# Row maxima turned by one matmul and placed by a transfer, loads as stages of the written schedule, a Newton root with a step less

## The reference, cut to what matters

```
x += tanh(g_xattn[0]) * matmul(fake_quant(layernorm(x)), fake_quant(ctx))
x += tanh(g_ffn[0])   * (h @ W_base.T + b + low-rank adapters through an inverse transform),  h = layernorm(x)
x += tanh(g_xattn[1]) * attention(layernorm(x), ctx)     # 32 query heads of 16, 8 key/value groups, masked softmax over 512 keys
x += tanh(g_ffn[1])   * bitlinear feed-forward(layernorm(x))   # int8-like activations, ternary weights, 512 -> 1376 -> 512
```

## Time and profile before

| | us |
|---|---|
| median of 3 runs | 267.83 (267.61 to 267.91) |
| the profiled execution, its own time | 267.79 |
| its span, first to last instruction | 266.0 |
| PE busy | 246.4 |
| DVE, ACT, POOL busy | 215.1, 185.3, 116.6 |

### The profile page before, as it was taken

One profiled execution on the slowest core, in us unless ns is written; L12 is line 12 of the kernel. 1 busy time (PEld: TensorE's weight loads), 2 busy tenths in 40 slices (PEclk: granted clock), 3 DMA queues, 4 the chain that ended last, 5 costly groups with the idle time before them and its releaser, 6 DMA issues.

```text
span 266.0 us, 4711 instructions
## 1 busy us (share of the span) xinstructions
PE 246.4 (93%) x1482; PEld 120.8 (45%) x1482; DVE 215.1 (81%) x613; ACT 185.3 (70%) x311; POOL 116.6 (44%) x172
## 2 busy tenths in 40 slices
PE   8957697979999999999999999999999999996994
PEld 8622275834733334275334266424334244443442
DVE  2976974779898589796999976899788995889995
ACT  3710549969498998487687767998878988543541
POOL 7003312562233022464888754447989668100000
PEclk9999799999999999999999999999999999999899
DMA  6999985152855800000900380630000000000004
GB/s 174 390 369 415 383 365 124 25 122 27 302 186 132 156 10 0 4 0 26 155 0 0 92 346 2 131 48 0 4 2 0 2 0 1 2 0 0 0 2 158
DMA packets 8146, 27.63 MB, mean 104 GB/s; under 512 B 1402, under 2 KB 4010, under 8 KB 6490
## 3 DMA queue, kind: packets, MB, share of 16 engines
q1 hardware_dynamic: 7690, 21.63, 27.8%
q0 software_dynamic: 288, 5.70, 5.6%
q10 hardware_dynamic: 144, 0.00, 0.0%
HBM read 23.87 MB, written 3.41 MB: 103 GB/s over the span
## 4 chain that ended last, share of the span: by engine, by line
PE 60%; DVE 8%; ACT 4%; issue 3%; DVEq 0%; ACTq 0%
PE bank L776 11%; PE bank L803 10%; PE bank L754 10%; PE bank L779 6%; PE bank L826 5%; PE bank L696 4%; PE bank L844 4%; PE bank L762 3%; PE bank L686 2%; PE bank L811 1%; DVE fs L1280 1%; ACT ternary L955 1%; PE bank L863 1%; ACT big L985 1%; PE bank L677 1%
## 5 line engine op out<-in xcount | busy, mean ns | idle before, releaser
L1215 DVE CUSTOM_DVE_ANT_0 junk<-bank,maskb 128x512 bf16<-128x512 f32 x128 | 83.8, 686 | 13.2 <-PE bank L754 12.8
L985 ACT ACTIVATE big<-bank 128x512 f32<-128x512 f32 x128 | 74.6, 597 | 20.4 <-PE bank L776 14.5
L562 POOL TENSOR_TENSOR big<-big,product 128x512 int32<-128x512 int32 x48 | 61.1, 1274 | 37.4 <-ACT big L985 36.9
L776 PE MATMUL bank<-qst,kst 99*128 99x512 bf16 x128 | 48.9, 383 | 0.2
L754 PE MATMUL bank<-kst,qst 96*128 96x512 bf16 x128 | 48.0, 381 | 0.2 <-DVE mx L1215 0.2
L803 PE MATMUL bank<-big,vp 128*32 128x512 f32 x256 | 30.6, 598 | 0.0
L779 PE MATMUL bank<-ident_b,maskb 128*128 128x512 bf16 x80 | 30.4, 380 | 0.0
L572 POOL TENSOR_TENSOR mx<-mx 128x4 f32<-128x4 f32 x64 | 14.1, 220 | 20.8 <-DVE mx L1215 18.6
L754 PEld LDWEIGHTS bank<-kst,qst 96*128 96x128 bf16 x128 | 12.7, 99 | 22.4 <-issue 12.8
L776 PEld LDWEIGHTS bank<-qst,kst 99*128 99x128 bf16 x128 | 12.4, 97 | 20.7 <-ACT big L985 7.9
L606 POOL TENSOR_SCALAR stage_w<-stage_w,wscale 128x1376 f32<-128x1376 f32 (+1 forms) x12 | 17.7, 1476 | 7.5 <-DVE wscale L1337 7.5
(11 more groups left out here) (183 smaller groups left out, 411.3 us busy)
## 6 DMA issues: line engine op xcount, KB each, us to landing
stage_w<-in_w_down POOLq DMA_DIRECT2D x1, 2816.0 KB, 9.9
stage_w<-in_w_gate SPq DMA_DIRECT2D x1, 2752.0 KB, 21.7
stage_w<-in_w_up POOLq DMA_DIRECT2D x1, 2752.0 KB, 10.3
qst<-q_parts SPq DMA_DIRECT2D x18, 128.0 KB, 4.8
q_parts<-parts SPq DMA_DIRECT2D x12, 128.0 KB
x<-in_x SPq DMA_DIRECT2D x4, 256.0 KB, 12.3
big<-in_ctx SPq DMA_DIRECT2D x4, 256.0 KB, 5.1
big<-in_ctxT SPq DMA_DIRECT2D x4, 256.0 KB, 7.2
```

What stands on the lines that cost most here:

```text
L562: nc.gpsimd.tensor_tensor(p, p, keep[:, nt, KEEP_ST.index(i):KEEP_ST.index(i) + 1, :].broadcast_to([P, HG, P]), ALU.mult).then_inc(kept, 1)
L776: i = mm(o[:, :], kst[0:KM, b, g, s * P:(s + 1) * P], qst[0:KM, tile % 2, g * HG:(g + 1) * HG, :], start=True, stop=by_keep(c, s))
L985: fn(pt[:, c % 4, s, :], o[:, :], ACT.Exp).then_inc(drain(stage), 1)
L1215: v.tensor_tensor_reduce(junk[:, j % 2, :], o[:, :], maskb[:, tb(c // NG)[1], :], 1.0, HIDE, ALU.add, ALU.max, mx[:, c % 3, 0, hh:hh + 1]) ...
```

## The change

Stage `m` becomes one matmul with 12 columns of weights (3 parts x 4 heads) into partitions 0 to 11 of a bank, 128 wide. ACT copies these 12x128 values into a new small tile `mrow` (three slots), and SP issues a transfer of 3 KB from there to rows `KS:KM` of `qst`; the first `t` of the chunk waits for that transfer (`max_placed`) and no longer for the copy. `m` moves to `j = 4c + 8` (`LAG_M = 8`) and `t` to a lag of 12. The identity is held once and read four times over by a broadcast.

The loads become stages of the list, each at a place of its own, some of them cut in pieces (`dft` in 2, `wT` in 4, batch 1's transposed context in 4). The stages that read the split queries and keys back are apart from their stores (`kstack`, `qstack`). The root takes two steps in place of three, the first of them of higher order: for one column 5 instructions and not 6, for three columns 7 and not 9. `oT` on DVE waits for the one before it. All stages are ordered anew.

```diff
-RSQRT_SEED = 519526879.0
+RSQRT_SEED = 520464379.0
+ROOT_G = -0.5 / (2.0 / 3.0) ** 0.4
...
-LAG_T = 11
+LAG_M = 8
+LAG_T = 12
 LAG_PV = 25
...
 PREPARATION = [
...
+    ("load_ctx", 2), ("load_x", 0), ("load_ctx", 0), ("warm", 0, 4, 10), ("load_ctx", 3), ("load_x", 3),
+    ("load_ctx", 1), ("load_x", 1), ("scalars",), ("load_enc",), ("warm", 0, 0, 42), ("load_ctxT", 0), ("products",),
+    ("xstats", 0), ("load_x", 2), ("ln0", 0, 1), ("ln0", 0, 2), ("ln0", 0, 3), ("ln0", 0, 4), ("load_dft", 1),
+    ("ln0", 0, 5), ("load_wkv",), ("load_dft", 0), ("xstats", 1), ("load_ctxT", 1), ("load_adapters",),
+    ("warm", 0, 1, 60), ("load_gate",), ("load_ctxT", 2), ("load_mask",), ("load_bias",), ("load_wT", 0),
+    ("cquant", 0), ("load_wT", 1), ("xstats", 2), ("xstats", 3), ("ln0q", 0), ("ln0", 1, 1), ("load_wT", 2),
+    ("load_wT", 3), ("load_ctxT", 5), ("ln0", 1, 2), ("ln0", 1, 3), ("k", 0, 0), ("load_ones",), ("csum", 0),
+    ("q1T", 0), ("k", 0, 1), ("ln0", 1, 4), ("vones",), ("adapters",), ("load_ctxT", 6), ("ln0", 1, 5), ("ln0q", 1),
+    ("r", 0), ("ln0r", 1), ("p", 0), ("vt",), ("ln1", 0, 0), ("ln0", 2, 5), ("load_ctxT", 4), ("ln1", 0, 1),
+    ("ln1", 0, 2), ("ln0q", 2), ("ln1", 0, 3), ("pick",), ("ln1", 0, 4), ("ln1", 0, 5), ("fabs", 0, 0), ("bias", 0),
+    ("fabs", 0, 1), ("we",), ("hT", 0, 1), ("mask",), ("fabs", 0, 2), ("fabs", 0, 3), ("fsum", 0), ("q1T", 1),
+    ("load_ctxT", 3), ("load_ctxT", 7), ("k", 0, 2), ("y0", 0, 0), ("y0", 0, 1), ("ln0r", 2), ("load_ctx", 4),
+    ("y0", 0, 2), ("y0", 0, 3), ("v", 0, 0), ("y0up", 0), ("fscale", 0), ("ln2", 0, 0), ("ln2", 0, 1), ("ln2", 0, 2),
+    ("r", 1), ("ln2", 0, 3), ("ln2", 0, 4), ("fround", 0, 0), ("load_wq",), ("v", 1, 0), ("ln2", 0, 5), ("k", 0, 3),
+    ("ksplit", 0), ("v", 1, 1), ("kstack", 0), ("k", 1, 0), ("p", 1), ("v", 1, 2), ("hT", 0, 2), ("ln1", 1, 0),
...
 FILL = {
...
+    12: [("bias", 2)], 14: [("qsplit", 1)], 15: [("hT", 2, 1)], 16: [("keepT",)], 17: [("y0", 2, 0)],
+    19: [("y0", 2, 1)], 21: [("y0", 2, 2)], 22: [("qstack", 1)], 24: [("y0", 2, 3), ("fabs", 1, 0)],
...
+    32: [("fround", 1, 0)], 33: [("fclamp", 1, 0), ("hT", 2, 2)], 35: [("load_wo",), ("oT", 0)],
...
+    56: [("fternary", 1, 1), ("y1", 0, 3), ("y1up", 0), ("hT", 3, 1)],
+    57: [("ln3", 0, 0), ("ln3", 0, 1), ("fternary", 1, 2)], 58: [("fternary", 1, 3)], 59: [("qstack", 2)],
+    61: [("fload", 2), ("ln3", 0, 2), ("y0", 3, 0)], 63: [("y0", 3, 1)], 64: [("ln3", 0, 3)], 65: [("y0", 3, 2)],
...
+    84: [("q", 3, 2), ("q", 3, 3), ("qsplit", 3), ("y1", 1, 0), ("y1", 1, 1)], 85: [("qstack", 3)],
...
+    179: [("hidden", 1, 2)], 217: [("oT", 7)], 224: [("y1", 3, 0)], 227: [("aT", 3, 1)], 277: [("fq", 0, 2)],
+    281: [("fq", 0, 3)], 288: [("y1", 3, 1)], 294: [("y1", 3, 2)], 296: [("y1", 3, 3)], 325: [("fq", 1, 0)],
+    334: [("f2T", 0, 0)], 341: [("y1up", 3)], 349: [("gu", 2, 0, 0)], 353: [("gu", 2, 0, 1)], 358: [("fq", 1, 1)],
...
+MROWS = 3
...
-        if (j - LAG_T + 1) % 4 == 0 and 0 <= (j - LAG_T + 1) // 4 < NCHUNK:
-            s.append(("m", (j - LAG_T + 1) // 4))
+        if (j - LAG_M) % 4 == 0 and 0 <= (j - LAG_M) // 4 < NCHUNK:
+            s.append(("m", (j - LAG_M) // 4))
...
+        mrow = sb("mrow", [3 * HG, MROWS, P], BF16)
...
+                elif kind == "m":
+                    c = stage[1]
+                    wait_drained(sp, stage)
+                    sp.dma_start(qst[KS:KM, c // NG % 2, c % NG * HG:(c % NG + 1) * HG, :],
+                                 mrow[:, c % MROWS, :]).then_inc(max_placed[c % MROWS], 16)
...
-                    for hh in range(HG):
-                        i = mm(o[KS:KM, hh * P:(hh + 1) * P], mx_top[:, c % 3, :, hh], ident_b[:, 0, :], start=True, stop=True)
-                    i.then_inc(fill(stage), 1)
+                    mm(o[0:3 * HG, 0:P], mx_top[:, c % 3, :, :].rearrange("p k h -> p (k h)"), ident_b[:, 0, :], start=True,
+                       stop=True).then_inc(fill(stage), 1)
...
-                        wait_drained(pe, ("m", c))
+                        pe.wait_ge(max_placed[c % MROWS], 16 * (c // MROWS + 1))
...
-                    fn(qst[KS:KM, c // NG % 2, c % NG * HG:(c % NG + 1) * HG, :],
-                       o[KS:KM, :].rearrange("p (h n) -> p h n", h=HG), ACT.Copy).then_inc(drain(stage), 1)
+                    if c >= MROWS:
+                        act.wait_ge(max_placed[c % MROWS], 16 * (c // MROWS))
+                    fn(mrow[:, c % MROWS, :], o[0:3 * HG, 0:P], ACT.Copy).then_inc(drain(stage), 1)
...
+                    if k == 3:
+                        link(which, v.scalar_tensor_tensor(out=y, in0=w, scalar=5.0 * ROOT_G ** 2, in1=y, op0=ALU.add, op1=ALU.mult))
+                        after(which)
+                    if k == 4:
+                        link(which, v.scalar_tensor_tensor(out=y, in0=u, scalar=1.5, in1=y, op0=ALU.add, op1=ALU.mult))
...
-                    after(which)
-                    link(which, v.scalar_tensor_tensor(out=y, in0=u, scalar=1.5, in1=y, op0=ALU.add, op1=ALU.mult))
+                    if k == 2:
+                        after(which)
+                        link(which, v.scalar_tensor_tensor(out=w, in0=u, scalar=-10.0 / 3.0 * ROOT_G, in1=u, op0=ALU.add, op1=ALU.mult))
...
```

More of the change, by code:

```diff
@@ L342, in gated_blocks_kernel @@
         ld_x = [sem(f"x_loaded{t}") for t in range(NT)]
-        ld_scal, ld_dft, ld_coef, ld_wT, ld_wq, ld_wkv, ld_wo, ld_mask, ld_bias = (
-            sem(n + "_loaded") for n in ("scalars", "dft", "coefs", "wT", "wq", "wkv", "wo", "mask", "bias"))
+        ld_scal, ld_coef, ld_wq, ld_wkv, ld_wo, ld_mask, ld_bias = (
+            sem(n + "_loaded") for n in ("scalars", "coefs", "wq", "wkv", "wo", "mask", "bias"))
         ld_enc = sem("enc_loaded")
+        ld_dft = [sem(f"dft_loaded{i}") for i in range(KT // 2)]
+        ld_wT = [sem(f"wT_loaded{k}") for k in range(KT)]
         enc_cleared = sem("enc_cleared")
@@ L348, in gated_blocks_kernel @@
         ld_ctx1 = sem("ctx1_loaded")
-        ld_ctxT0 = [sem(f"ctxT0_loaded{k}") for k in range(KT)]
-        ld_ctxT1 = sem("ctxT1_loaded")
+        ld_ctxT = [sem(f"ctxT_loaded{i}") for i in range(B * KT)]
         ld_ffn = [sem(f"ffn_loaded{w}") for w in range(3)]
@@ L388, in gated_blocks_kernel @@
         max_split = sem("max_split")
+        max_placed = [sem(f"max_placed{i}") for i in range(MROWS)]
         pv_done = sem("pv_done")
@@ L457, in _ @@
-            sp.dma_start(dft, dft_in).then_inc(ld_dft, 16)
-            sp.wait_ge(enc_cleared, 1)
-            for half in range(2):
-                sp.dma_start(enc[64 * half:64 * half + RR, :], enc_in).then_inc(ld_enc, 16)
-            sp.dma_start(wT[:, :, :], wT_in).then_inc(ld_wT, 16)
-            sp.dma_start(bias[:, :], bias_in.partition_broadcast(P)).then_inc(ld_bias, 16)
-            for t in range(1, NT):
-                sp.dma_start(x[:, t, :], x_in[:, t, :]).then_inc(ld_x[t], 16)
@@ L465, in _ @@
-            sp.dma_start(wqT[:, :, :], wqT_in).then_inc(ld_wq, 16)
-            sp.dma_start(mask_u8, mask_in).then_inc(ld_mask, 16)
-            sp.dma_start(ctx_T[:, 1], ctxT_in[1]).then_inc(ld_ctxT1, 16)
-            sp.dma_start(ctx_n[:, 1], ctx_in[1]).then_inc(ld_ctx1, 16)
-            sp.wait_ge(minus_ready, 1)
-            for b in range(B):
-                sp.dma_start(kst[KS:KM, b, :, :], minus.broadcast_to([KM - KS, NG, SK])).then_inc(kones_ready, 16)
-            sp.dma_start(stage_w[:, 0:WFF[0][1]], WFF[0][0]).then_inc(ld_ffn[0], 16)
@@ L473, in _ @@
-            sp.dma_start(woT[:, :, :], woT_in).then_inc(ld_wo, 16)
-            for stage in SCHEDULE:
-                kind = stage[0]
-                if kind in ("ksplit", "qsplit"):
+            for stage in SCHEDULE:
+                kind, i = stage[0], (stage[1] if len(stage) > 1 else 0)
+                if kind == "load_x":
+                    sp.dma_start(x[:, i, :], x_in[:, i, :]).then_inc(ld_x[i], 16)
+                elif kind == "load_ctx":
+                    if i < KT:
+                        sp.dma_start(ctx_n[:, 0, i], ctx_in[0, :, i]).then_inc(ld_ctx0[i], 16)
+                    else:
+                        sp.dma_start(ctx_n[:, 1], ctx_in[1]).then_inc(ld_ctx1, 16)
+                elif kind == "load_ctxT":
+                    sp.dma_start(ctx_T[:, i // KT, i % KT], ctxT_in[i // KT, :, i % KT]).then_inc(ld_ctxT[i], 16)
+                elif kind == "load_wkv":
+                    sp.dma_start(wkvT, wkvT_in).then_inc(ld_wkv, 16)
+                elif kind == "load_adapters":
+                    sp.dma_start(coef, coef_in).then_inc(ld_coef, 16)
+                    sp.dma_start(cmask, cmask_in).then_inc(ld_coef, 16)
+                elif kind == "load_dft":
+                    sp.dma_start(dft[:, 2 * i:2 * i + 2], dft_in[:, 2 * i:2 * i + 2]).then_inc(ld_dft[i], 16)
+                elif kind == "load_enc":
+                    sp.wait_ge(enc_cleared, 1)
+                    for half in range(2):
```

(20 more changed lines are left out.)

78 lines of the change are left out of this document (33 added, 45 removed), and 86 rows, old and new, of tables (FILL, PREPARATION).

## The result

The changed kernel takes 271.14 us (median of 4, 270.22 to 271.79), the kernel before 267.72 (median of 4, 267.43 to 267.91): a ratio of 1.0113, 95% interval 1.0079 to 1.0146. Foretold were 261.7 us, range 255.0 to 268.5.

The account below looks back on a forecast made before the run. Bounds taken: loads and long chains up to the first score, PE in the loop, a DVE chain at the end. From 267.79 us: -5.5 + 1.5 + 3.0 + 0.5 - 4.6 - 1.0 = -6.1, so 261.7 us, range 255 to 268.5.

Parts of the forecast that it names:

- the one on SP's queue: Loop: the maxima's transfer stands behind whatever SP issues or waits for; 3.0 us lost, bounds 0 and 6.
- The four matmuls: Stage `m` in the loop: three matmuls fewer in each of 32 chunks, 5.5 us saved, bounds 5.5 and 11.3.
- The new wait in twelve short windows: Loop: `t` waits for copy and transfer where four steps are as short as that path; 1.5 us lost, bounds 0 and 10.
- The reads behind the stores: Loop, after `qstack` 1, 2, 3: transfers behind six query reads land late; 0.2 + 1.5 + 1.9 us, within the 3.0 taken.
- One step less for `keep`: Loop: `t` is a step later and `pv` is not, leaving `keep` less room; 0.5 us lost, bounds 0 and 2.
- The preparation: Up to the first score matmul: reordered loads bring it to 57.5 us; 4.6 us saved in all, bounds -8 and +1.
- The root and the end: Last norm and tail: shorter root 0.2 us, `gu 2` fills PE's wait; 1.0 us saved in all, bounds -3 and +2.
- The slower one: Rival, loop: small transfer takes 3.9 us, each of 12 short windows loses 1.5; 274.7 us, chance 0.14.
- The rival in which the loop gives all back: Rival: loop waits reach 9 or 10 us, or the first score stays at 62.5; 266.2 or 266.3 us, chance 0.15.

Follow-up runs that it names:

- the run with the old lag: Changed kernel with maxima placed by four matmuls and a copy, and LAG_M, LAG_T = 10, 11 as before the change: 276.03 us, ratio 1.0294 to the kernel before.
- the kernel with 72 columns: Changed kernel with the one matmul of the maxima widened from 12 to 72 columns of weights, 60 of them zeros: 268.10 us, ratio 0.9997 to the kernel before.

## Why the prediction was wrong

**The step that failed is the one on SP's queue, in this sentence:** "The 2.75 MB of `fload` come on another queue and share the engines." It was priced at nothing, as if a share of the engines were all that a small transfer needs. The transfer landed 6.54 and 5.64 us after issue, about when the load was in, and not the 2.1 of the sum: 3.20 and 2.71 us of waits at the two places, and 4.8 us of low clock behind them, by loads that are not in SP's queue. With the loads cut to 128 columns the kernel takes 262.1 us. So 9.1 us are this one step, the low clock included. The sentence named the collision and did not put the two in order of time: `fload` in steps 11 and 61, ten microseconds or eight steps of it, and an `m` every four.

That 262.1 is next to the forecast of 261.7 is partly luck. In the profile of that run the way to the first score is 3.8 us shorter than before (foretold 4.6), the loop 1.8 shorter (foretold 0.5), the end 0.3 longer (foretold 1.0 shorter): the misses cancel.

**The low clock had no term.** The prediction counted a microsecond of PE's waiting as one. Here 5.9 us of waiting in two places took 4.8 more with them. The rows of before had such a case at the end: a clock of 0.83 between 240 and 250 us beside PE's gaps.

**The four matmuls.** Right: 0.057 apart, 0.09 on either side left in place. That the 0.09 belongs to the form of the tile was a bound of the sum (11.3 for 5.5); the runs show that it can be had by widening, 5.9 us of PE's time, of which 3.0 reached the median. The Trainium skill, page "TensorEngine Tiling (Array Packing)", Key Properties, says that a change of tiling mode drains the engine; here that is 0.09 in and 0.10 out, and nothing where the mode stays.

**The new wait in twelve short windows.** 1.5 foretold, and it isn't there. The path was sized too long, 3.4 us: the shortest room from an `m` to its `t` is 3.4 us, as worked out, but where nothing disturbs the transfer the path takes 2.3 to 2.5, of which 1.75 from issue to landing (2.1 in the sum). PE and SP in a short window, with no wait before `t`; the transfer had landed at 207.73:

```profile
205.43 0.22 PE L790 MATMUL bank<-ident_b,mx 128*12 128x128 bf16 x1
...
205.98 0.70 SPq L539 DMA_DIRECT2D qst<-mrow  x1
...
208.88 0.39 PE L803 MATMUL bank<-qst,kst 99*128 99x512 bf16 x1
```

Other waits of the loop took 1.8 us more than before.

**The reads behind the stores.** 3.0 us for three places; there is one, 0.78, where `m`'s transfer is issued behind the reads of `qstack 3`:

```profile
174.62 6.02 SPq L539 DMA_DIRECT2D qst<-mrow  x2
...
180.23 0.39 PE L803 MATMUL bank<-qst,kst 99*128 99x512 bf16 x1 [0.78 <-DMA qst<-mrow]
```

The mechanism was right: this transfer landed 5.57 us after issue, as late as those beside the loads, and 8.6 behind the first read, where the prediction had 8. It cost less because PE had 6.3 us of work between this `m` and its `t`, where it had 3.5 at the second load. The other two places show no wait.

**One step less for `keep`.** 0.5; PE's waits for it are 1.0 us. The mechanism was right, and its size within the bounds.

**The preparation.** Right: the first score at 57.1 for 57.5, with the work behind `y0 0` begun at 33.1 for 32.4 and 0.7 us of waits in it for 1.8. What was missed is that the order which wins this gives it back: with the maxima placed directly, the loop took 4.4 us more than before at nearly the same matmuls. How much of that is `keep` and how much the other work that moved behind the first score stays open; the run with the old lag was to tell, and mixed in a third wait.

**The root and the end.** The root is worth 0.3 (0.2 foretold). PE's wait for the last `hq` fell from 2.19 to 1.43, and the end is 55.7 us long, where 55.4 were, so +0.3 in place of -1.0. What took it back is seen in PE's waits there, 4.4 us in sum for 2.9: 1.4 for `hid` of DVE and 1.3 for ScalarE have come up.

**The rivals.** The slower one had the right transfer and the wrong cause: it made it slow by itself, 3.9 us to landing in twelve windows. It takes 1.75 by itself and is late where something big is under way. The rival in which the loop gives all back had waits of 9 or 10 us, and the loop's waits for the transfer and the others are 9.6; its 266.2 lacks the 4.8 of the low clock.

## To carry over

A small transfer on the path is priced by what is under way when it is issued: lay its issue times over those of every load, on whatever queue, and give it up to what the load still has. Reads on its own queue count as much: six of them took it to 5.57 us. Loads that can wait are issued in pieces at different times; pieces issued together changed next to nothing here. And a wait of PE of some 3 us is counted with the slower clock that may follow it.

## What the runs showed of the hardware

- A transfer of 12 pieces of 256 B lands 1.75 us after issue in an empty stretch. It took 6.5 and 5.7 us to release its reader while a load of 2.75 MB from another queue was under way, and 5.6 behind six reads on its own. Neither four pieces in place of one (waits of 2.53 and 2.63) nor another issuing engine (3.50 and 3.38) changed it.
- Behind waits of 3.20 us, of 2.71 and of 2.05 PE ran at 1.2 GHz for 6.4, 3.4 and 3.4 us (the last two begin about 1 us behind the wait); behind one of 3.38 (the kernel with 72 columns, its matmuls from 81.98 on 0.22 apart) it didn't. So the rows don't give a length from which it falls.
- SP takes 0.70 us to issue such a transfer, ScalarE 0.73, though 3 KB are moved; the 2.75 MB of gate weights took SP 0.49.
- A matmul with 12 columns of weights costs 0.19 us more than one with 72 between full ones, and four with 99 columns start 0.055 us apart, as four with 3 do.
